# A fused vision-text layer on one core: three groups of instructions reordered on ScalarE and VectorE

## The reference

```python
h = concatenate([tokens(x), txt], axis=1)            # (16, 193, 128)
h = h + attention(layernorm(h))
y = layernorm(h)
shared = silu(y @ sw1) * (y @ sw3) @ sw2
scores = y @ gate_w.T
_, idx = top_k(scores + biases, 2)                   # which experts
topv, _ = top_k(scores, 2)                           # their weights
p = sigmoid(topv); p = p / p.sum(-1)
h = h + sum_k p[k] * expert[idx[k]](y) + shared
```

## Time and profile before

| what | value |
|---|---|
| time, median of 3 runs | 254.12 us (253.86 to 258.68) |
| profiled execution, first to last instruction (span) | 252.9 us |
| PE busy | 226.1 us (89%) |
| DVE busy | 189.9 us (75%) |
| ACT busy | 155.6 us (62%) |
| POOL busy | 114.1 us (45%) |

### The profile page before, as it was taken

The page is one execution under the profiler, slowest core; times in us unless marked ns, Lnnn a source line. Parts: engine busy times, 40 slices in busy tenths (PEclk is TensorE's granted clock), DMA queues, the critical chain, the costliest instruction groups (busy, mean ns, idle before and its releaser), DMA issues.

```text
span 252.9 us, 5578 instructions
## 1 busy us (share of the span) xinstructions
PE 226.1 (89%) x1483; PEld 189.7 (75%) x1483; DVE 189.9 (75%) x739; ACT 155.6 (62%) x438; POOL 114.1 (45%) x121
## 2 busy tenths in 40 slices
PE   3878989999999999978989979999999999999930
PEld 2857778979898989856576557888888888887720
DVE  3537887998989898998986877766666666665892
ACT  3045577676867676858963165666666666666390
POOL 1400000074838383812666702666666666666400
PEclk9999997999999999999999999999999999999995
DMA  6999964061607110100102421414233333329577
GB/s 202 352 352 352 319 210 170 0 222 35 232 22 235 32 43 24 42 21 13 54 33 83 99 66 33 119 55 118 84 87 93 85 88 86 91 75 278 137 179 190
DMA packets 31565, 31.68 MB, mean 125 GB/s; under 512 B 4338, under 2 KB 27419, under 8 KB 30768
## 3 DMA queue, kind: packets, MB, share of 16 engines
q1 hardware_dynamic: 27240, 24.57, 32.9%
q0 software_dynamic: 3392, 6.36, 7.7%
q10 hardware_dynamic: 904, 0.41, 0.6%
HBM read 22.80 MB, written 9.03 MB: 126 GB/s over the span
## 4 chain that ended last, share of the span: by engine, by line
PE 69%; DVE 16%; ACT 5%; SPq 3%; issue 3%; DMA 2%; DVEq 0%; ACTq 0%
PE bank L1616 15%; PE bank L1636 10%; PE bank L1329 8%; PE bank L1625 5%; PE bank L1535 3%; DMA xp_both<-in_patches 2%; PE bank L1605 2%; PE bank L1520 2%; PE bank L1412 2%; PE bank L1523 2%; PE bank L1398 2%; DVE sh_h L1099 2%; PE bank L1374 2%; PE bank L1350 2%; PE bank L1432 2%
## 5 line engine op out<-in xcount | busy, mean ns | idle before, releaser
L812 POOL DMA_INDIRECT xs_dram<-xd,pos_i x50 | 55.0, 1100 | 69.8 <-DVE pos_i L1001 57.0
L823 POOL DMA_INDIRECT y_dram<-att,goal x56 | 55.1, 984 | 36.8 <-ACT att L749 36.5
L1329 PE MATMUL bank<-wt,xp_both 128*128 128x128 f32 x288 | 39.8, 291 | 7.0 <-DMA xp_both<-in_patches 7.0
L1329 PEld LDWEIGHTS bank<-wt,xp_both 128*128 128x128 f32 x288 | 37.4, 203 | 8.4 <-DMA xp_both<-in_patches 5.6
L735 ACT ACTIVATE att<-bank 128x256 f32<-128x256 f32 x56 | 21.5, 384 | 24.4 <-PE bank L1616 24.4
L1636 PE MATMUL bank<-w_sb,att 128*128 x224 | 34.5, 276 | 0.0
L1236 DVE CAST xsT_h<-bank 128x128 fp32r<-128x128 f32 x56 | 16.3, 291 | 24.1 <-PE bank L1605 24.0
L1636 PEld LDWEIGHTS bank<-w_sb,att 128*128 128x128 f32 x224 | 29.4, 191 | 0.3 <-issue 0.2
L1616 PE MATMUL bank<-xp_both,xsT_h 128*128 x56 | 26.8, 479 | 0.7 <-DVE xsT_l L1238 0.7
L1249 DVE TENSOR_TENSOR att<-att,bank 128x256 f32<-128x256 f32 x56 | 23.0, 410 | 1.7 <-ACT att L735 1.7
L1616 PE MATMUL bank<-xp_both,xsT_l 128*128 x56 | 22.2, 396 | 0.0
(11 more groups left out here) (210 smaller groups left out, 497.0 us busy)
## 6 DMA issues: line engine op xcount, KB each, us to landing
xp_both<-in_patches SPq DMA_DIRECT2D x6, 1152.0 KB
xs_all<-xs_dram SPq DMA_DIRECT2D x56, 64.5 KB, 1.8
xd<-y_dram SPq DMA_DIRECT2D x8, 384.0 KB, 5.1
w<-in_w SPq DMA_DIRECT2D x2, 1024.0 KB, 10.3
y_dram<-att,goal POOLq DMA_INDIRECT x56, 2.3
xs_dram<-xd,pos_i POOLq DMA_INDIRECT x50
xp_both<-in_patches SPq DMA_DIRECT2D x1, 768.0 KB, 5.7
hrow<-in_txt SPq DMA_DIRECT2D x2, 384.0 KB, 8.0
```

The source lines that it names most:

```text
L812: nc.gpsimd.indirect_dma_start(out=xs_dram[:, :], out_offset=bass.IndirectOffsetOnAxis(ap=pos_i[0:rows, j, k:k + 1], axis=0), in_=xd[0:row ...
L823: nc.gpsimd.indirect_dma_start(out=y_dram[:, :], out_offset=bass.IndirectOffsetOnAxis(ap=goal[u][:, 0:1].bitcast(I32), axis=0), in_=ys[u][ ...
L1329: M(ps[:, 0:D], xp[p][:, k, :], wt[:, k, :], start=(k == 0), stop=False)
```

## The change

Nothing is added to the computation or taken from it; instructions change places on ACT and DVE. There are three parts. In pass 1, ACT's `norm2(0)` comes ahead of the text roots and the text rows. In passes 1 to 6, DVE's `turn(i)` comes ahead of `patch_rows(i + 1)`. The raw maxima of all groups are taken behind the last group's choice, among the shared expert's products, and their combination stands two products later than before.

```diff
--- before.py
+++ after.py
@@ -634,11 +634,13 @@
                 centre_tap(i)
                 rstd2(i - 1)
                 if i == 1:
+                    norm2(i - 1)
                     rstd_texts(3, 2, 4)
                 if i == 3:
                     rstd_texts(4, 4, G)
                 norm_texts(i + 1)
-                norm2(i - 1)
+                if i > 1:
+                    norm2(i - 1)
                 queries(i)
                 columns2(i - 1)
                 rstd1(i + 1)
@@ -966,8 +968,6 @@
                                      gateb_sb[:].rearrange("p (o e) -> p o e", o=1).broadcast_to([P, n, E]), ALU.add))
                 for j in tiles:
                     last = V.max(mx8[:, j, :], scb[:, j, :])
-                if g < G - 1:
-                    raw_best(g)
                 then(last)
                 for j in tiles:
                     last = V.max_index(ix8[:, j, :], mx8[:, j, :], scb[:, j, :])
@@ -1085,8 +1085,8 @@
                 if i == 3:
                     mean_texts(4, 4, G)
                 turn_parts(i)
+                turn(i)
                 patch_rows(i + 1)
-                turn(i)
                 patch_stats(i + 1)
                 tap_before(i)
 
@@ -1176,16 +1176,9 @@
             then(V.tensor_copy(tf[:], ti[:, 1, :]))
             shared_mul(4, 0)
             shared_add(3)
-            raw_best(G - 1)
-            then(V.tensor_tensor(swap[:], ix8[:, :, 0], ix8[:, :, 1], ALU.is_gt))
-            dve.wait_ge(raw_done, J)
-            then(V.tensor_scalar(keep[:], swap[:], -1.0, 1.0, ALU.mult, ALU.add))
-            best = raw8[:, :, 0:2].rearrange("p j k -> p k j")
-            V.tensor_tensor(part[:, 0], best, keep[:].rearrange("p (k j) -> p k j", k=1).broadcast_to([P, 2, J]), ALU.mult)
-            then(V.tensor_tensor(part[:, 1], best[:, ::-1, :], swap[:].rearrange("p (k j) -> p k j", k=1)
-                                 .broadcast_to([P, 2, J]), ALU.mult))
-            V.tensor_tensor(by_slot[:], part[:, 0], part[:, 1], ALU.add).then_inc(top_done, 1)
             shared_mul(4, 1)
+            raw_best(0)
+            raw_best(1)
             V.tensor_scalar(t_w[:], tf[:], float(-P), float(CAP), ALU.mult, ALU.add)
             then(V.tensor_tensor_scan(te[:], cst[:, C_ONES:C_ONES + E], tf[:], 0.0, ALU.mult, ALU.add))
             tile_no, tile_row = cst[:, C_TILE:C_TILE + 1], cst[:, C_TILE + 1:C_TILE + 2]
@@ -1198,11 +1191,22 @@
             remainder_w13(6)
             shared_add(4)
             shared_mul(5, 0)
+            raw_best(2)
             dve.wait_ge(cols_turned, 1)
             V.tensor_copy(tab[:], bank[6][0:1, 0:2 * TILES].rearrange("p (k t) -> p k t", k=2)).then_inc(tab_done, 1)
+            for g in range(3, G):
+                raw_best(g)
             shared_mul(5, 1)
             remainder_w13(7)
             shared_mul(EARLY, 0)
+            then(V.tensor_tensor(swap[:], ix8[:, :, 0], ix8[:, :, 1], ALU.is_gt))
+            dve.wait_ge(raw_done, J)
+            then(V.tensor_scalar(keep[:], swap[:], -1.0, 1.0, ALU.mult, ALU.add))
+            best = raw8[:, :, 0:2].rearrange("p j k -> p k j")
+            V.tensor_tensor(part[:, 0], best, keep[:].rearrange("p (k j) -> p k j", k=1).broadcast_to([P, 2, J]), ALU.mult)
+            then(V.tensor_tensor(part[:, 1], best[:, ::-1, :], swap[:].rearrange("p (k j) -> p k j", k=1)
+                                 .broadcast_to([P, 2, J]), ALU.mult))
+            V.tensor_tensor(by_slot[:], part[:, 0], part[:, 1], ALU.add).then_inc(top_done, 1)
             shared_mul(EARLY, 1)
             for k in range(2):
                 last = V.tensor_scalar(t_n[:, k, :], cst[:, C_BUF:C_BUF + U], te[:, E - 2 + k:E - 1 + k], None, ALU.add)
```

## The result

The changed kernel takes 260.48 us (median of 4 runs, 259.55 to 263.27), the kernel before 255.87 beside it (253.86 to 258.68): a ratio of 1.0253, 95% interval 1.0209 to 1.0296. The change makes the kernel slower by more than 2%, and the forecast of 256.1 with its range up to 257.8 was wrong. The profiled execution took 259.74, its span is 257.9: 5.0 us over the span of before.

A forecast was written before the change was run, and what follows sets the result against it. TensorE was taken to bound the kernel, with 69% of the chain, so other engines' moves count only where it waits. Norm 1.23, patch statistics 0.78 and scores 0 sum to +2.0 on 254.12: 256.1 us, range 254.0 to 257.8.

The forecast's parts named there:

- The norm moved ahead: Pass 1: the 1.19 us wait before the transposes goes, but the late text mean delays the turn and `sums(1)`; +1.23 us.
- I take +1.2, half clock as before: Pass 1 clock: half clock stays as long as before, so `sums(1)` ending its stage 1.23 us later counts in full.
- upper bound of +2.3: Pass 1 norm term if half clock lasts that much longer than before.
- 1.23 - 1.1 = +0.1: Pass 1 norm term if the changed kernel keeps 2.4 GHz there, the lower bound.
- Rival (a): Pass 1: the wait goes and nothing replaces it; with the patch statistics -0.3, 253.8 us; chance 0.06.
- The patch statistics: Passes 2 to 6: later statistics delay the key masks that `attend` loads; 0.22 + 4 x 0.14 = +0.78 us.
- "Issue": Profile's name for idle time before `attend`'s weight load; read as the wait for the masks, 0.22 us behind their end.
- rival (b): Before `attend`: the "issue" time is TensorE's own; 1.23 - 0.4 = +0.8, 254.9 us; chance 0.12.
- The scores: Shared expert's stretch: the 21 moved MAX, 1.5 to 1.9 us, just fill VectorE's waits of 1.74; taken as 0.
- (c): Around 40 us: the clock stays at 2.4 GHz; 0.1 + 0.78 = +0.9, 255.0 us; chance 0.12.
- (d): At 151 us: longer idle before the first expert transposes brings another clock fall, 1.6 lost; +3.6, 257.7 us; chance 0.10.
- The chance of 0.04 for slower by over 2%: Whole kernel: chance of being over 2% (5.1 us) slower, given for (d) with every upper end.

The follow-up runs named there:

- the norm alone: Kernel before with only group 0's second norm put ahead of the text roots in pass 1: 259.02 us, ratio 1.0183.
- The scores alone: Kernel before with only the raw maxima and the combination of the scores moved behind the last group's choice: 254.43 us, ratio 0.9998.
- the patch rows alone: Kernel before with only patch rows and statistics put behind the rotary turn's sum: 256.05 us, ratio 1.0018.
- the repaired order: Kernel before with the norm moved ahead and VectorE's text mean of that pass put behind the turn's first products: 255.99 us, ratio 1.0005.
- the same with the repair: Changed kernel with the text mean put behind the turn's first operations in the first pass: 256.36 us, ratio 1.0081 against the kernel before.
- the same with the filler: Changed kernel with 11 extra matmuls on TensorE between the first group's second transposes and the rotary sum: 257.52 us, ratio 1.0125 against the kernel before.

## Why the prediction was wrong

**The norm moved ahead: the mechanism right, the term mis-sized.** Predicted and measured: transposes at 37.05 and 37.18, text mean at 37.40 and 37.50, `sums(1)` at 40.33 and 40.45, idle stretch 2.7 and 2.72. The trace of after starts 0.08 late, so the chain through VectorE came out to 0.1. The step that failed is "I take +1.2, half clock as before", with its upper bound of +2.3: by the norm alone the term is +3.31. Three things were wrong in it.

- Half clock was counted from the start of `sums(1)`: 2.2 us of it for at most 1.1, and for the bound twice as long, 2.2. It lasted 6.7 us behind that start (40.45 to 47.14), over `sums(1)` and both halves of attention, all on the chain, and taking it away alone gave back 2.69. That is 0.40 for each us, where the working had 0.50: the length failed, and not the price.
- The baseline was one execution with a fall in it. The scores alone and the patch rows alone have the same 1.19 us and no fall there. Without any fall the text mean's delay costs 29.21 - 27.54 = 1.67; against the profile of before that is 1.67 - 1.05 = +0.62, where my working had 1.23 - 1.1 = +0.1. The whole term is 1.67 + 2.69 - 1.05 = 3.31. The mean granted clock on record for every run tells how common such a baseline is: it is 0.987 to 0.989 in the profiled executions without a fall ahead of the last slices, 0.981 and 0.982 in those with one fall of 3.4 us. Of the 74 executions of the kernel before beside the experiments 31 have 0.985 or more.
- The start of `sums(1)` was taken from the chain (39.10, the end of the transposes). The timeline has it at 38.90, so it moved by 40.45 - 38.90 - 0.08 = 1.47 and not by 1.23. This is 0.2 of the 0.52 between +0.1 and +0.62.

**Rival (a)** falls with the text mean, and the repaired order shows that beside an execution without a fall it had no gain to offer: the 1.19 us turn into a wait for the turn's sum.

**The patch statistics: right.** Predicted +0.78 (0.22, then 4 times 0.14). The part alone has 0.36 by the third group and 0.63 over the next four, +0.99; on top of the norm, in the changed kernel, it has 0.12 and 0.54 (the four passes take 50.96 against 50.42 for the norm alone), +0.66. "Issue" in front of the weight load was the wait for the masks, and rival (b) falls.

**The scores: right by themselves.** The first expert transposes came 4.01 late, the work at 108 us 4.12 (108.57 to 112.69): nothing was added between, although their combination now stands four products later, and not two as the section on the change says. What the move does is to lengthen the idle time ahead of the experts.

**Rivals (c) and (d).** (c) went the other way: the clock fell for longer. (d), one more fall at the experts, came, and the sum had nothing for it: behind 1.01 us of idle time, below the 1.19 from which I let it decide. The four traces with 1.01 to 1.06 us there are those with the scores moved; three of them have the fall, at 152 to 156 us (the changed kernel, the same with the repair, the same with the filler), the scores alone do not. None of the eight with 0.65 us or less has it. So the longer idle time goes with this fall, though not each time; all three also have the patch rows behind the turn, and no run parts the two. Behind the first transposes the three spans with it last 103.7 to 103.9 us, the nine without 102.8 to 103.2: it costs 0.5 to 1.0, against a price of 1.6.

The 5.0 us of the profiled span: 0.08 start, 3.43 up to the third group's attention, 0.61 in the next four passes, -0.11 to the experts, 0.99 behind them, with the fall there. The first three make 4.12, already past the range's upper end (257.8 is +3.7). The chance of 0.04 for slower by over 2% came from a range whose clock term was bounded too tightly, and which left the fall at the experts to a rival.

## What to carry to other kernels

When a step is moved ahead on one engine, look on every other engine for an in-order instruction that waits for a step it overtook, and move that too; here one line on VectorE was worth 1.8%, the clock behind it included. Where a change lengthens TensorE's idle stretch on the chain, price the half clock behind it over everything that runs there until the clock is back, and not by a single earlier fall; filling the stretch with matmuls that fit is a cheap test of that price. And read the clock of several executions before taking a fall into the baseline.

## What the runs showed of the hardware that was not expected

- An idle stretch of 1.19 us on TensorE was followed by 1.2 GHz in the profile of before, and not in those of the scores alone and the patch rows alone. Behind 1.05 and 0.89 us (the two repaired orders) it was not either. Behind 2.72 and 2.79 us it was, in both traces that have it (6.8 us at half clock). With the stretch filled to 0.27 and 0.34 it was not. The other falls ahead of the last slices lasted some 3.4 us each. What decides between falling and not stays open.
- All four profiles with the patch rows behind the turn have at least one fall between 108 and 240 us, and two of the eight others. Whether the slower passes bring that on was not tried; it may explain why the repaired changed kernel is 0.8% slower where the patch rows alone are 0.2%.
